# A Mamba block over 16 images: a later, regrouped order of the preparation stages, a state ring of eight, B and C spread by DMA, and u = dt x from SBUF

## The reference, cut to what matters

```
x = x + L0(gn(x))     # every pixel: its nearest of 256 words (cosine) replaces it where close enough
x = x + L1(gn(x))     # layer norm, a Mamba block on each quarter of the channels, layer norm, projection

# the Mamba block, for each image and each of 4 chunks of 64 channels (d: 128 inner channels, s: 16 states)
xi, z = split(x @ in_proj_w.T)
xc = silu(depthwise_conv4(xi) + conv_b)
dt, B, C = split(xc @ x_proj_w.T)             # 4, 16 and 16 columns
dt = softplus(dt @ dt_proj_w.T + dt_proj_b)
h[t] = exp(dt[t] * A) * h[t-1] + (dt[t] * xc[t]) * B[t]      # 128 x 16 states, over 1024 pixels
y[t] = sum_s h[t] * C[t];  y = (y + xc * D) * silu(z)
out = y @ out_proj_w.T
```

## Time and profile before

| | us |
|---|---|
| median of 3 runs | 5035.2 |
| lowest and highest | 5031.6, 5037.42 |
| the profiled execution, its own time | 5045.31 |
| its span in the trace | 5043.5 |
| mean granted TensorE clock | 0.866 of full speed |

### The profile page before, as it was taken

The page is one execution under the profiler, slowest core; times in us unless marked ns, Lnnn a source line. Parts: engine busy times, 40 slices in busy tenths (PEclk is TensorE's granted clock), DMA queues, the critical chain, the costliest instruction groups (busy, mean ns, idle before and its releaser), DMA issues. The chain is left out here.

```text
span 5043.5 us, 50728 instructions
## 1 busy us (share of the span) xinstructions
PE 4261.0 (84%) x13584; PEld 1366.9 (27%) x13584; DVE 4235.7 (84%) x3517; ACT 2601.2 (52%) x3272; POOL 3470.8 (69%) x2101
## 2 busy tenths in 40 slices
PE   3888988888888888988888888888888889888887
PEld 2222323222232222322223232222322223222221
DVE  2688888888888889888888888888888898888886
ACT  2455555554555455455555555555454554555542
POOL 2667767667677766767667676676777667676664
PEclk8798888888898898988888888888988989888887
DMA  1446454554645546455554645546455464555543
GB/s 45 121 131 160 123 141 123 150 145 123 155 117 150 136 128 166 117 142 130 148 150 119 151 112 150 146 125 155 111 152 136 128 166 116 142 130 148 146 129 99
DMA packets 193349, 676.10 MB, mean 134 GB/s; under 512 B 23192, under 2 KB 25056, under 8 KB 189024
## 3 DMA queue, kind: packets, MB, share of 16 engines
q1 hardware_dynamic: 193120, 673.10, 51.7%
HBM read 572.34 MB, written 67.11 MB: 127 GB/s over the span
## 5 line engine op out<-in xcount | busy, mean ns | idle before, releaser
L558 POOL TENSOR_TENSOR state<-state,c_all 128x1024 f32<-128x1024 f32 x1024 | 2411.2, 2358 | 1249.0 <-DVE state L931 1228.6
L931 DVE TENSOR_TENSOR_SCAN state<-dtb,ub 128x1024 f32<-128x1024 f32 x1024 | 2339.2, 2284 | 57.5 <-PE yp L1156 15.0
L1140 PE MATMUL ub<-u,spr 32*128 32x512 f32 x4096 | 1363.2, 747 | 615.7 <-DVE state L931 605.9
L734 ACT ACTIVATE dtb<-dtb,a_neg 128x1024 f32<-128x1024 f32 x1024 | 1164.6, 1142 | 368.0 <-DMA dtb<-dt_scratch 365.9
L922 DVE TENSOR_TENSOR ub<-ub,b_all 128x1024 f32<-128x1024 f32 x1024 | 1242.6, 1213 | 98.4 <-PE ub L1140 63.9
L1140 PEld LDWEIGHTS ub<-u,spr 32*128 32x128 f32 x4096 | 350.7, 209 | 1512.6 <-DVE state L931 1100.6
L1156 PE MATMUL yp<-state,gat 128*32 128x512 f32 x4096 | 627.2, 688 | 4.9 <-POOL state L558 4.9
L1023 PE MATMUL mb<-xs,wtap 128*128 128x512 f32 x512 | 335.2, 814 | 32.7 <-DVE cd L911 22.2
L633 ACT ACTIVATE dt<-mb 128x512 f32<-128x512 f32 x128 | 76.3, 596 | 551.1 <-PE mb L1043 551.1
L822 DVE TENSOR_TENSOR u<-mb,xc 128x512 f32<-128x512 f32 x128 | 88.4, 691 | 289.1 <-ACT dt L633 288.7
L608 ACT ACTIVATE e_x<-mb,ncb 128x512 f32<-128x512 f32 x128 | 87.5, 683 | 260.5 <-PE mb L1023 260.5
(11 more groups left out here) (137 smaller groups left out, 5140.7 us busy)
## 6 DMA issues: line engine op xcount, KB each, us to landing
dtb<-dt_scratch SPq DMA_DIRECT2D x1024, 512.0 KB, 4.7
xs<-xn SPq DMA_DIRECT2D x128, 256.0 KB, 5.7
xt<-in_x SPq DMA_DIRECT2D x16, 1024.0 KB, 7.0
x_scratch<-xt SPq DMA_DIRECT2D x16, 1024.0 KB, 6.8
dt_scratch<-dt SPq DMA_DIRECT2D x64, 256.0 KB, 3.4
dt_scratch<-dt SPq DMA_DIRECT2D x128, 128.0 KB, 3.3
res<-x_scratch SPq DMA_DIRECT2D x16, 1024.0 KB, 10.0
out<-res SPq DMA_DIRECT2D x16, 1024.0 KB, 7.7
```

What stands on the lines that cost most here:

```text
L558: pool.tensor_tensor(v, v, c_all[:, c % 2, :], ALU.mult).then_inc(gated, 1)
L734: act.activation(dtb[:, k, :], dtb[:, k, :], ACT.Exp, scale=a_neg[:, GROUP[g]:GROUP[g] + 1]).then_inc(decayed, 1)
L931: dve.tensor_tensor_scan(state[:, k, :], dtb[:, k, :], ub[:, g % 2, :], 0.0, ALU.mult, ALU.add).then_inc(scanned, 1)
L1140: last = pe.matmul(ub[:, g % 2, h * HALF:(h + 1) * HALF], spr[lo:lo + 32, GROUP[g] % 4, :], u[lo:lo + 32, c % 2, h * HALF:(h + 1) * HALF], ...
```

## The change

It rebuilds the order and some of what is ordered:

- Nearly every stage has another place in the tables. The state ring has STATES = 8 slots, apart from the ring of dtb, which stays at 4; PE sums a pair three steps later (BEHIND = 5: at an odd g the pair g-5, g-4).
- B and C: two matmuls with 32 output rows each (prep_bc) in place of four with 128; ACT copies both to a small tile bcs, SP stores it to HBM (two stores of 64 KB) and loads it back spread over the partitions (two loads of 512 KB for a chunk). DVE and POOL wait for these loads in place of seq_ready.
- dt: each half's four matmuls are split in two pairs (prep_part, prep_dt). The bank is freed by ACT after its copy.
- u: DVE reads the tile dt, ACT's copy in SBUF, and not the bank. PE waits for u (u_done) ahead of the first spread of a chunk, and ACT waits for the u before ahead of overwriting dt.
- z: made in the chunk it belongs to and not one chunk ahead (own_z), one tile zz.
- post_out handles both pixel halves at one place of each chunk, and yy shares the memory of ll; res shares that of xn, so that the read-back x2_back waits for the chunk loads xs, and the stage a_xn for the output store.
- The pixel norms of L0 sum their two squares in PE (32 small matmuls for 16) and not on POOL (a_squares is gone).

```diff
-LAG = 2
+STATES = 8
+BEHIND = 5
...
-DVE_SEQ = {4: ["post_gate"], 8: ["post_skip0"], 9: ["post_skip1"], 20: ["prep_u0"], 21: ["prep_u1"]}
+DVE_SEQ = {9: ["post_gate"], 24: ["prep_u0"], 25: ["prep_u1"]}
...
-SP_SEQ = {22: ["prep_store"]}
+SP_SEQ = {19: ["prep_bc_store"], 22: ["prep_bc_load"], 23: ["prep_store"]}
...
+            def store_bc(m, par):
+                await_(bc_copied, 2 * m + 2)
+                for h in range(2):
+                    sp.dma_start(bc_s[par, :, h * HALF:(h + 1) * HALF],
+                                 bcs[32 * h:32 * h + 32, :]).then_inc(s_bcst, 16)
+            def load_bc(m, par):
+                await_(s_bcst, 32 * (m + 1))
+                await_(bx_done, 16 * (m - 1))
+                await_(gated, 16 * (m - 1))
+                for dst, first, done in ((b_all, 0, s_ball), (c_all, NS, s_call)):
+                    src = bc_s[par, first:first + NS, :].unsqueeze(1).broadcast_to((NS, 8, L))
+                    sp.dma_start(dst[:, par, :], src).then_inc(done, 16)
...
                 if name == "x2_back":
                     await_(s_x2st, 16 * b)
+                    for q in range(NC):
+                        await_(s_xs[q], 32 * (NB if kind == "tail" else b + 1))
...
                 elif name in ("prep_dt0", "prep_dt1"):
                     at_least(act, s_dtst, 48 * m)
+                    at_least(act, u_done, 2 * m)
                     bank, use = banks(kind, b, (name, c))
                     act.wait_ge(m_full[bank], use)
                     act.activation(dt[:, cut], mb[:, bank, :], ACT.Copy).then_inc(dt_copied, 1)
+                    act.wait_ge(dt_copied, 2 * m + h + 1)
+                    act.sem_inc(m_free[bank], 1)
...
-                    bank, use = banks(kind, b, (f"prep_dt{h}", c))
                     dve.wait_ge(dt_copied, 2 * m + h + 1)
-                    dve.tensor_tensor(u[:, par, cut], mb[:, bank, :], xc[:, par, cut], ALU.mult).then_inc(m_free[bank], 1)
+                    dve.tensor_tensor(u[:, par, cut], dt[:, cut], xc[:, par, cut], ALU.mult).then_inc(u_done, 1)
...
-                at_least(dve, summed, n - RING + 1)
-                dve.tensor_tensor_scan(state[:, k, :], dtb[:, k, :], ub[:, g % 2, :], 0.0,
+                at_least(dve, summed, n - STATES + 1)
+                dve.tensor_tensor_scan(state[:, g % STATES, :], dtb[:, k, :], ub[:, g % 2, :], 0.0,
...
-                            if g > LAG:
-                                sum_pair(b, c, g - LAG - 1)
+                            if g >= BEHIND:
+                                sum_pair(b, c, g - BEHIND)
```

More of the change, by code:

```diff
@@ L85 @@
+SP_BATCH = {(0, 4): ["x_in"], (0, 15): ["xs3"], (0, 17): ["x2_back"], (2, 3): ["x2_store"], (2, 8): ["out"],
+            (2, 13): ["xs0"], (2, 17): ["xs1"], (2, 19): ["out_wait"], (3, 15): ["xs2"]}
 FIRST, LOOP, LAST = "first", "loop", "last"
@@ L215, in build @@
         xn = sb("xn", [P, NJ, L])
+        res = xn
         hot_t = sb("hot_t", [P, 2, L], BF16)
@@ L659, in do @@
                     act.wait_ge(dt_exp, m + 1)
-                    at_least(act, z_silu, m)
+                    at_least(act, z_silu, m - 1)
                     act.activation(e_z[:], e_x[:], ACT.Identity, bias=1.0).then_inc(dt_one, 1)
                 elif name == "prep_dt_ln":
+                    if kind != "pro" and not (kind == FIRST and c == 0):
+                        for q in range(2):
+                            bank, use = banks(kind, b, (f"post_out{q}", c))
+                            act.wait_ge(m_full[bank], use)
                     act.activation(ll[:], e_x[:], ACT.Ln, bias=1.0).then_inc(dt_ln, 1)
@@ L685, in do @@
                         act.wait_ge(x2_done, NJ * (t + 1))
-                        at_least(act, s_xs[3], 32 * t)
-                    act.activation((xn if g else cd)[:, j, :], xt[:, j, :], ACT.Square, scale=gsm[:, 4, j:j + 1],
+                        if kind not in ("pro", FIRST):
+                            for q in range(2):
+                                bank, use = banks(kind, b, (f"c_proj1{q}", 0))
+                                act.wait_ge(m_full[bank], use)
+                    act.activation(cd[:, j, :], xt[:, j, :], ACT.Square, scale=gsm[:, 4, j:j + 1],
                                    bias=gsm[:, 5, j:j + 1])
@@ L1025, in do @@
                     last.then_inc(m_full[bank], 1)
[L1026 to L1029 removed]
+                elif name == "own_z":
+                    for q in range(2):
+                        bank = enter(kind, b, (f"own_z{q}", c))
+                        lo = DM * q
+                        first = PAD + q + q * HALF
+                        pe.matmul(mb[:, bank, :], wz[lo:lo + DM, :], xs[lo:lo + DM, c, first:first + HALF],
+                                  start=True, stop=True).then_inc(m_full[bank], 1)
                 elif name.startswith("prep_raw"):
@@ L1061, in do @@
                     if h == 0:
-                        pe.wait_ge(sq_added, t + 1)
+                        pe.wait_ge(a_sqd[0], NJ * (t + 1))
                         enter(kind, b, (name, 0))
                     for i in range(h * NT // 2, (h + 1) * NT // 2):
-                        last = pe.matmul(mb[:, bank, i:i + 1], cd[:, 0, i * P:(i + 1) * P], onef[:],
-                                         start=True, stop=True)
+                        for j in range(NJ):
+                            last = pe.matmul(mb[:, bank, i:i + 1], cd[:, j, i * P:(i + 1) * P], onef[:],
+                                             start=(j == 0), stop=(j == NJ - 1))
                     if h == 1:
@@ L1204, in _ @@
             turn(LAST, NB - 1)
-            sum_pair(NB - 1, NC - 1, NU - 2)
-            for name in ["post_out0", "post_out1"] + C_STATS + C_PROJ:
+            for g in range(NU + 1 - BEHIND, NU, 2):
+                sum_pair(NB - 1, NC - 1, g)
+            for name in ["post_out"] + C_STATS + C_PROJ:
                 do(name, "tail", NB, 0)
```

216 lines of the change are left out of this document (111 added, 105 removed), and 32 rows, old and new, of tables (ACT_BATCH, DVE_BATCH, PE_BATCH).

## The result

| | before | changed kernel |
|---|---|---|
| median, us | 5036.3 (4 runs, 5031.6 to 5040.7) | 4833.5 (4 runs, 4822.6 to 4845.0) |
| the profiled execution, its own time | 5045.3 | 4845.0 |
| its span | 5043.5 | 4843.1 |
| mean granted TensorE clock | 0.866 | 0.829 |

The ratio is 0.9598, with a 95% interval of 0.9574 to 0.9622: faster by 4.0%, or 203 us. The forecast was 4690 in a range of 4550 to 4860. So the sign and the wide range held, but the time lies above the forecast's own range of 4620 to 4800, and the forecast was 143 us too low: 203 us came of the 346.

What follows compares the result with a forecast made beforehand. DVE was taken to pace the steps, idling 664 of 4850 us. Gains of 225, 131, 57 and 15 (428) less losses of 8 and 74 (82) gave net 346: 5035 to 4690 us, own range 4620 to 4800, wide range 4550 to 4860.

Steps and rivals of the forecast that it cites:

- dt and u, removed: DVE's waits for dt in the steps go, 249 us, less 24 where x2_back makes ACT late: 225 us gained.
- The output projection: DVE's waits for ym go, since its three stages now stand at least a step apart: 131 us gained.
- u from SBUF: Each chunk's first product u waits 1.15 us for POOL's running gate, the second 0: 74 us lost.
- Rival (a): u beside POOL costs nothing and ACT is never late for the dt copy: 4590 us; chance 27%.
- (b): Each product u waits for a whole POOL gate, 302 us in place of 74: 4920 us; chance 5%.
- B and C through HBM, SP's queue: New loads and stores of B and C, and unit loads behind the dt stores, land in time: 0.
- rival (d): Stores of dt queue behind the new B and C loads and stall the next chunk: 5230 us, slower; chance 5%.
- What PE must do in time: PE's work fits the 4.6 us between two spreads; the conv's place stays, ub's 63.9 us are kept: 0.
- rival (c): PE runs dt at 1.2 GHz, 3.6 us over its room in 64 chunks, 230 us: 4920 us; chance 8%.
- Statistics and similarity: DVE meets rs and sim a step later, so 57 us of their waits go; 8 us lost in mixing stages.
- State ring and later sum: DVE's waits for state slots go, with 8 slots and the sum five steps behind: 15 us gained.
- The sum: All terms together: 428 us gained, 82 lost, net 346 us.

Runs made afterwards that it cites:

- e2_u_early: Changed kernel with the first product u moved from behind multiply 12 to behind scan 11; 4842.6 us, ratio 0.9609.
- e4_before_u: Kernel before with one edit: the product u reads the tile dt in SBUF and not the bank; 5116.4 us, ratio 1.0153.
- e3_xc_split: Changed kernel with the second half of the conv on PE one place later, behind the next spread; 4803.1 us, ratio 0.9538.
- e10_xc_early: e1_u_bank with the conv's first half at PE's place 3 and its second at place 5, where both stood; 4808.1 us, ratio 0.9549.
- e9_full_rows: Changed kernel with one extra 128-row matmul ahead of the spreads of steps 14, 15 and 0 to 3; 4893.2 us, ratio 0.9715.
- e11_sim_early: e10_xc_early with L0's second pixel-norm half and first similarity stage one place earlier on PE in chunk 0; 4798.8 us, ratio 0.9525.
- e5_behind3: Changed kernel with BEHIND = 3 in place of 5, so PE sums a pair two steps earlier, ring of 8 kept; 5538.7 us, ratio 1.1006.
- e1_u_bank: Changed kernel, but DVE reads the product u's input from the bank and frees it, as before; 4784.4 us, ratio 0.9500.
- e6_warm: Changed kernel with the spreads of steps 14, 15 and 0 to 3 of each chunk issued twice; 4995.4 us, ratio 0.9929.

## Why the prediction was right, and where it failed

**dt and u, removed: right.** Forecast 225 us gained, of 289 us. All of it that lies in the steps went; the 24 us set aside for x2_back, which makes ACT late, weren't needed.

**The output projection: right.** Forecast 131, measured 129 (133.9 to 4.5).

**u from SBUF: right.** Forecast 74 us as 64 times 1.15 us, measured 81 (169.7 less 88.4). The picture of the first product holds: it comes while a gate runs, and takes 1.95 us in most chunks. The price of 0 for the second came for a reason that the forecast did not have. It was to start together with the gate of step 12; but that gate starts 2.4 us later (2124.82), behind the clamp of z, and the product runs beside an idle POOL (0.66 us). In the second chunk of nearly every image POOL lags, and the two take 1.8 and 1.05 us. The rule of the Trainium skill (SBUF — State Buffer, Who interferes with whom), by which the first to issue has the shared port for its whole instruction, is borne out by the first product's end behind the gate's and, from the other side, by the gate of 2.73 us behind a product in e2_u_early. Rival (a), that nothing collides, is refuted, and so is (b), a whole gate every time, although single products of 2.70 us occur where the order allows it (e4_before_u).

**B and C through HBM, SP's queue: right at 0.** DVE doesn't wait for dtb, and rival (d) is refuted. Of the marks set for the forecast only DVE's share fell short: 89% in place of above 90.

**What PE must do in time: here it failed.** The sentence was "That place stays as it is, so I keep all of ub's 63.9 us". It doesn't stay as it is. The conv itself stays between the spreads of the steps 3 and 4, but in the kernel before the product with silu(z) stood at DVE's place 4 and ran just as PE began the conv. Its timeline of DVE there:

```profile
2220.25 1.22 DVE L798 TENSOR_TENSOR yy<-yp,zz 128x1024 f32<-128x1024 f32 x1
...
2227.70 1.23 DVE L922 TENSOR_TENSOR ub<-ub,b_all 128x1024 f32<-128x1024 f32 x1 [0.60 <-PE ub L1140]
```

The hole was 0.60 us there and is 2.25 us where the product has gone to place 9. In this chunk the product accounts for 1.2 us of the difference and the slower conv for up to 0.7. I had priced the moved product by who waits for it, and not by what its 1.2 us on DVE had covered. In the first chunks of the images the conv takes some 5.4 us before and 5.5 after, and there the wait grew from almost nothing to 1.9 us: two stages of L0's statistics on DVE, which stood at places 3 and 5, have gone to 9 and 10 too. That the conv's place is a cause is shown by e3_xc_split (50 us of waits at step 4 and 30 us of time go) with e10_xc_early (split elsewhere it doesn't pay). The product itself can't be put back to place 4, as the last sum of a chunk now comes at step 3 of the next.

The waits for ub with their "issue" gaps grew from 83 to 179 us, 96 us of the 126 that are missing in the idle time. Added up by the step of the multiply that waits, the conv's place is only a third of it:

| step | before, us | after, us |
|---|---|---|
| 0 | 38.4 | 32.2 |
| 4, behind the conv | 41.4 | 72.2 |
| 9, behind the second half of prep_raw | 0 | 18.3 |
| 11, behind the first pair of dt's terms | 0 | 45.6 |
| all others | 3.4 | 10.7 |

The larger part lies in the step where dt is made. PE and DVE there, in the third chunk of an image:

```profile
1222.83 1.94 PE L1197 MATMUL yp<-state,gat 128*32 128x512 f32 x8
1224.69 2.08 PE L1080 MATMUL mb<-rl,idf 128*128 128x512 f32 x2
1226.56 1.92 PE L1081 MATMUL mb<-ll,idf 128*128 128x512 f32 x2
1228.40 1.13 PE L1181 MATMUL ub<-u,spr 32*128 32x512 f32 x4
```

```profile
1229.58 1.23 DVE L954 TENSOR_TENSOR ub<-ub,b_all 128x1024 f32<-128x1024 f32 x1 [3.08 <-PE ub L1181]
```

At 2.4 GHz a dt matmul takes 1.02 to 1.13 us and the sum 1.07. Here they take twice that, the granted clock of the stretch from 1216 to 1228 is 0.50 with PE busy for all of it (it was 1.00 from 1196 to 1214, at whose end PE idled four times for 0.6 to 1.2 us), and the spread of step 11 comes 3.1 us late. It happens in 15 of the 64 chunks (10 first and 5 third ones). The budget of 4.6 us between two spreads was reckoned at the full clock.

The same step said that "PE's total falls a little", and drew from it that nothing gets worse. PE's busy time fell (4261.0 to 4159.2), but so did the granted clock, from 0.866 to 0.829; e9_full_rows shows that of the conv's 314.7 us some 66 hang on that clock.

So rival (c), PE at its low level in dt, came true in a quarter of the chunks, at 45.6 us in place of 230. The argument against it was that the second half of dt always ran fast. That is so in both kernels; but in the kernel before the first half's first matmul took 2.1 us in some 40 chunks by PE's timeline, and the earlier trace rows show the second half alone. Its mark, ub waits above 150 us, was reached only with the gaps counted in (179). No run changes dt's place or its clock by itself, so this part is read from the trace and not tested.

**Statistics and similarity: mis-sized.** Forecast 57 us gained, measured 7 by the waits for PE (119.8 to 112.9), and nothing by all idle time ahead of the two (122.2 to 123.7). I had let the waits go because DVE meets these stages a step later. But PE reaches them later too: the first of the similarity stages is waited for 2.3 us once an image, at the start of PE's block of 12 matmuls for them (L1120, x24 in its rows), which begins at 2264.45. This timeline of DVE shows it:

```profile
2268.24 0.88 DVE L882 TENSOR_SCALAR sim<-mb,rn 128x256 f32<-128x256 f32 x2 [2.31 <-PE mb L1120]
```

By e11_sim_early it isn't free to take away either: the same PE time is then asked for at the next spread.

**State ring and later sum: right in size, wrong in kind.** The 15 us of waits for its slots went, though all idle time ahead of the scan fell by only 6.1 (57.5 to 51.4). But the later sum isn't a separate small gain; without it the new order is 10% slower than the kernel before (e5_behind3).

**The sum, closed.** Counted as all idle time ahead of an instruction, whoever ended it, DVE idles less ahead of u (250.0 us), of the output projection's addition (128.5), of rs (15.3), of the scan (6.1) and of the rest (3.8); it idles more ahead of the multiply (93.0) and of sim (16.8). That is 293.9 us less; with 93.5 more of work it makes 200.4, the difference of the two spans. The forecast had 420 and 74.

**The range held, and in part by luck.** Its upper end of 4860 was set for the unknown price of u, which came out at 81 us against 74. What filled that room was something else, the waits for ub, which stood in the sum with 0, and those at rs and sim.

**What is open.** It is open how much of the lower clock is due to the z and the B and C matmuls. They now overlap in pairs (below) and so no longer keep PE busy as long with the same work; no run takes this alone. In the order before, neither the larger ring of states nor the later sum was tried alone, nor was an order in which the whole conv stands beside the product with silu(z).

## What to carry to other kernels

When a stage is moved, price it twice: by who waits for it at the new place, and by what ran in its shadow at the old one. Reckon what fits between two steps at the lower clock too, where rows show that stage at either level, and look at every chunk's place and not at one: the chunk shown above had its dt at the full clock. An elementwise product with both inputs in SBUF costs what is left of the GpSimd instruction that is running when it is issued, and the profile shows this as a longer product and not as a wait; leaving one input in PSUM avoids it. With two engines both near 90% busy, a stall taken away paid only a part of its length here: 49 us of 83 in e1_u_bank, 30 of 65 in e3_xc_split.

## What the hardware showed that was not expected

- PE ran without a gap and stayed at the low level. After 11 us of spreads (32 rows) and sums (32 columns) back to back, the conv's four matmuls took 5.56 us in e6_warm; with 128x128 matmuls between the same spreads they took 3.70 us in e9_full_rows. The levels are 1.2 and 2.4 GHz. The Trainium skill (TensorE: Matmul & The Clock Gate, What's actually happening) says that the clock is set by how busy PE has been lately; the second run agrees, the first does not in a stretch that the profile shows as wholly busy.
- Two float32 matmuls that use different parts of the array run beside each other. z's two matmuls, which both took the array's first 64 rows, needed 1.99 us in the kernel before; one on the first and one on the last 64 rows, they need 1.13. The two of B and C, now on 32 columns each, need 1.05 us, where two of B's with 128 columns took 1.98. PE's timeline of the changed kernel:

```profile
2120.78 1.13 PE L1064 MATMUL mb<-xs,wz 64*128 64x512 f32 x4
...
2167.66 1.05 PE L1074 MATMUL mb<-xc,wbc 128*32 128x512 f32 x4
```

- The wait of DVE and POOL for each other works both ways. POOL's gate grew to 2.73 us behind a product of 0.67 us, and a product grew to 2.70 us behind a gate of 2.36.
